# Two-layer graph attention on one core: the head's order of x, W and wh, and who makes the low parts in the two closings

## The reference, cut to what matters

```python
def layer(x, W, adj):                    # x (4096, 256), W (256, 512), adj (4096, 4096)
    Wh, Ws = split(x @ W, 2, axis=-1)
    a = softmax(Wh @ Ws.T, axis=-1) * adj
    return leaky_relu(a @ Wh + x, 0.01)
y = x
for l in range(2):
    y = layer(y, W_stack[l], adj)
out = layernorm(x + y)                   # over the last axis, eps 1e-5
```

## Time and profile before

| what | us |
|---|---|
| median of 3 runs | 1600.88 (1599.6 to 1602.52) |
| the profiled execution | 1602.16, span 1600.4 |
| TensorE busy | 1556.9 (97% of the span) |
| VectorE busy | 1349.2 (84%) |
| GpSimd busy | 800.8 (50%) |
| ScalarE busy | 646.9 (40%) |
| mean granted TensorE clock | 0.994 |

### The profile page before, as it was taken

One profiled execution on the slowest core, in us unless ns is written; L12 is line 12 of the kernel. 1 busy time (PEld: TensorE's weight loads), 2 busy tenths in 40 slices (PEclk: granted clock), 3 DMA queues, 4 the chain that ended last, 5 costly groups with the idle time before them and its releaser, 6 DMA issues.

```text
span 1600.4 us, 23327 instructions
## 1 busy us (share of the span) xinstructions
PE 1556.9 (97%) x8104; PEld 1320.4 (83%) x8104; DVE 1349.2 (84%) x1569; ACT 646.9 (40%) x1175; POOL 800.8 (50%) x801
## 2 busy tenths in 40 slices
PE   6999999999999999999899999999999999999996
PEld 6888888888888888888787888888888888888875
DVE  4688778877887788788847899999999999999988
ACT  4344444344444444443434444443344444444432
POOL 0055555555555555555422555555555555555554
PEclk9999999999999999999899999999999999999999
DMA  5277767676777777678924777787777777777784
GB/s 190 75 189 192 198 184 201 185 202 188 199 191 197 195 192 200 190 200 210 240 92 120 197 194 211 191 202 189 206 197 205 197 207 198 194 208 195 203 221 119
DMA packets 166981, 302.57 MB, mean 189 GB/s; under 512 B 39760, under 2 KB 67408, under 8 KB 166736
## 3 DMA queue, kind: packets, MB, share of 16 engines
q1 hardware_dynamic: 104896, 131.97, 32.6%
q0 software_dynamic: 37200, 135.28, 29.6%
q10 hardware_dynamic: 24768, 33.85, 7.8%
HBM read 157.29 MB, written 9.44 MB: 104 GB/s over the span
## 4 chain that ended last, share of the span: by engine, by line
PE 88%; DVE 6%; DMA 2%; issue 1%; SPq 1%; ACT 1%; POOL 1%; ACTq 0%; POOLq 0%
PE banks L634 27%; PE banks L521 16%; PE banks L523 15%; PE banks L522 15%; PE banks L636 14%; DVE ring L958 2%; SPq L348 1%; DVE ring L963 1%; DVE x_t L894 1%; DVE neg_max L930 1%; DMA turned<-ring 1%; POOL a_lo L1128 1%; DMA ring<-x_scratch 0%; PE banks L564 0%; ACT ring L764 0%
## 5 line engine op out<-in xcount | busy, mean ns | idle before, releaser
L1128 POOL TENSOR_TENSOR a_lo<-turned,a_hi 128x512 fp32r<-128x512 f32 x488 | 627.4, 1301 | 626.1 <-ACT a_hi L785 624.2
L634 PE MATMUL banks<-wh,a_hi 128*128 128x512 f32 x1952 | 700.0, 398 | 7.1 <-POOL a_lo L1128 6.9
L764 ACT ACTIVATE ring<-banks,neg_max 128x1024 f32<-128x1024 f32 x256 | 286.1, 1118 | 850.0 <-DVE neg_max L930 839.0
L636 PE MATMUL banks<-wh,a_lo 128*128 128x256 f32 x1952 | 548.8, 281 | 0.0
L930 DVE TENSOR_REDUCE neg_max<-banks 128x1 f32<-128x1024 f32 x256 | 311.9, 1219 | 166.8 <-PE banks L523 166.8
L634 PEld LDWEIGHTS banks<-wh,a_hi 128*128 128x128 f32 x1952 | 367.8, 188 | 96.9 <-POOL a_lo L1128 7.1
L521 PE MATMUL banks<-x_t,q_t 128*128 128x512 f32 x1024 | 407.7, 398 | 6.8 <-DVE q_t L894 6.8
L523 PE MATMUL banks<-x_t,q_t 128*128 128x512 f32 x1024 | 402.9, 393 | 0.0
L522 PE MATMUL banks<-x_t,q_t 128*128 128x512 f32 x1024 | 401.0, 392 | 0.0
L636 PEld LDWEIGHTS banks<-wh,a_lo 128*128 128x128 f32 x1952 | 369.4, 189 | 7.9
L958 DVE SCALAR_TENSOR_TENSOR ring<-ring,weight,load 128x1024 f32<-128x1024 f32 x254 | 328.4, 1293 | 0.8 <-DMA load<-adj 0.7
(11 more groups left out here) (81 smaller groups left out, 895.7 us busy)
## 6 DMA issues: line engine op xcount, KB each, us to landing
load<-adj POOLq DMA_DIRECT2D x254, 512.0 KB, 5.1
turned<-ring SPq DMA_DIRECT2D x1504, 64.0 KB, 4.0
turned<-ring ACTq DMA_DIRECT2D x496, 64.0 KB, 3.2
ring<-x SPq DMA_DIRECT2D x8, 512.0 KB, 5.8
rows<-x SPq DMA_DIRECT2D x32, 128.0 KB, 3.4
x_scratch<-rows SPq DMA_DIRECT2D x32, 128.0 KB, 2.9
rows<-x_scratch SPq DMA_DIRECT2D x30, 128.0 KB, 3.5
first_rows<-x SPq DMA_DIRECT2D x30, 128.0 KB, 3.1
```

The costliest lines, as they stand in the source:

```text
L634: nc.tensor.matmul(psum[:, bank, :], of_hi[:, b], wh[:, k].rearrange("p a d -> p (a d)"), start=start, stop=stop, skip_group_check=True)
L636: last = nc.tensor.matmul(psum[:, bank, 0:D], of_lo[:, b], wh[:, k, 0], start=False, stop=stop, skip_group_check=True)
L764: nc.scalar.activation(ring_at(i).rearrange("p (r b j) -> p b r j", r=2, j=QUAD), psum[:, 2 * (i % 2):2 * (i % 2) + 2, :].rearrange("p h ( ...
L1128: nc.gpsimd.tensor_tensor(operand(1, j).rearrange("p b (r j) -> p b r j", r=QUADS), as_f32(turned_in[unit_place(unit)][:, :, b:b + SUB, :] ...
```

## The change

Head: SyncE loads W of layer 0 and seven groups of x at once (two into `load`), the eighth when W's first half is split, W of layer 1 when group 4 has been turned. TensorE turns groups 0 to 5 through three pairs of banks with `q` 0 after group 2; groups 6 and 7 come after the first scores, W of layer 1 is turned in step 1 and its M made in step 2. Its parts lie in the last four tiles of `wh` until they are stored. GpSimd loads the first adj when groups 5 and 6 are turned. wh: two per step, in steps 0 to 7 (layer 0) and 4 to 7 (layer 1).

Closings: VectorE's low parts are 1, 2, 3, 5, 7 (layer 0) and 1, 2, 3 and the other odd ones (layer 1), each placed between a weighing and its turning. Chunk 125's maximum is taken before weigh 121, 126's before turn 122. GpSimd waits for weigh 124 before low 4, for weigh 125 before low 6, and for weigh 127 before low 8.

```diff
+        FIRST_BANKS = [0, 2, 6, 0, 2, 6, 2, 6]
+        FIRST_FREE = [0, 0, 0, 1, 2, 3, 5, 6]
-        LOW_BY_DVE = [(0, 1, 3), tuple(range(1, 16, 2))]
+        LOW_BY_DVE = [(1, 2, 3, 5, 7), (1, 2, 3, 5, 7, 9, 11, 13, 15)]
+        def head_at(step):
+            return {0: [("x", 6), ("x", 7)], 1: [("wt", 1)], 2: [("w", 1)]}.get(step, [])
-        WH_AFTER = [{0: 3, 1: 3, 2: 3, 3: 3, 4: 2, 5: 2}, {3: 3, 4: 3, 5: 2}]
+        WH_AFTER = [{n: 2 for n in range(8)}, {n: 2 for n in range(4, 8)}]
...
-            for g in range(2):
+            for g in range(GROUPS - 1):
                 load_x(g)
+            sp.wait_ge(wt_done, 1)
+            sp.wait_ge(w_lo, 1)
+            load_x(GROUPS - 1)
+            sp.wait_ge(xt_done, 5)
             load_w(1)
-            for g in range(2, 4):
-                load_x(g)
-            for g in range(4, GROUPS):
-                sp.wait_ge(xt_done, g - 3)
-                load_x(g)
...
             transpose_x(1)
-            pe.wait_ge(wt_lo, 1)
-            transpose_w(1)
             transpose_x(2)
-            make_m(1)
-            for g in range(3, GROUPS):
+            make_side(("q", 0))
+            for g in range(3, 6):
                 transpose_x(g)
-            pe.wait_ge(wt_lo, 2)
-            make_side(("q", 0))
...
                 scores(chunk_at(step))
+                for kind, n in head_at(step):
+                    if kind == "x":
+                        transpose_x(n)
+                    elif kind == "wt":
+                        pe.wait_ge(xt_lo, GROUPS)
+                        transpose_w(n)
+                    else:
+                        make_m(n)
...
-            def last_steps(end, last):
+            def last_steps(end, j, last):
                 weigh_and_turn(end - 9)
                 row_weights(last - 1)
                 chunk_max(end - 4)
                 weigh_and_turn(end - 8)
+                chunk_max(end - 3)
                 weigh_and_turn(end - 7)
-                chunk_max(end - 3)
-                weigh_and_turn(end - 6)
+                weigh(end - 6)
                 chunk_max(end - 2)
+                turn_blocks(end - 6)
+                weigh_and_turn(end - 5)
+                finish_rows(last - 3)
+                chunk_max(end - 1)
+                low_a(j + 1)
+                row_weights(last)
+                low_a(j + 2)
+                weigh(end - 4)
+                low_a(j + 3)
+                turn_blocks(end - 4)
+                weigh(end - 3)
+                low_a(j + 5)
+                turn_blocks(end - 3)
             def close_first():
...
-                low_a(j)
-                low_a(j + 1)
-                row_weights(TILES - 1)
-                weigh_and_turn(CHUNKS - 4)
-                low_a(j + 3)
-                weigh_and_turn(CHUNKS - 3)
                 split_x(8)
-                weigh_and_turn(CHUNKS - 2)
+                weigh(CHUNKS - 2)
+                low_a(j + 7)
+                turn_blocks(CHUNKS - 2)
                 weigh_and_turn(CHUNKS - 1)
             def close_second():
...
-                weigh_and_turn(end - 4)
-                low_a(j + 3)
-                weigh_and_turn(end - 3)
-                low_a(j + 5)
-                weigh_and_turn(end - 2)
-                low_a(j + 7)
+                weigh(end - 2)
+                low_a(j + 7)
+                turn_blocks(end - 2)
                 weigh_and_turn(end - 1)
...
-            pool.wait_ge(w_next_stored, 32)
             for i in range(2):
+                pool.wait_ge(xt_done, GROUPS - 2 + i)
                 load_adj(nc.gpsimd, i)
...
             def close_first():
-                split_a(j + 2)
+                split_a(j)
                 load_next_x(10)
                 load_last_adj(end)
-                for n in range(4, 12):
+                for n in (4, 6):
+                    pool.wait_ge(a_done, end - 4 + n // 2 - 1)
                     split_a(j + n)
                 pool.wait_ge(a_done, end)
+                for n in (8, 9, 10, 11):
+                    split_a(j + n)
...
             def close_second():
                 split_a(j)
-                split_a(j + 2)
                 load_last_adj(end)
-                split_a(j + 4)
-                split_a(j + 6)
+                for n in (4, 6):
+                    pool.wait_ge(a_done, end - 4 + n // 2 - 1)
+                    split_a(j + n)
                 load_late_rows()
+                pool.wait_ge(a_done, end)
                 split_a(j + 8)
```

More of the change, by code:

```diff
@@ L310, in gat_layernorm @@
             last_in[side_bank[s]] = side_place[s]
-        x_rows = [ring[:, g % 4, :] for g in range(GROUPS)]
+        x_rows = [ring[:, n, :] for n in (0, 1, 2, 3, 5)] + [load[:, 0, :], load[:, 1, :], ring[:, W_SLOT, :]]
         x_rows += [as_f32(q_t[:, p]).rearrange("p a k n -> p (a k n)") for p in range(2)]
@@ L317, in gat_layernorm @@
         x_rows += [ring_at(X_CHUNK[14]), ring_at(X_CHUNK[15])]
-        x_place = [g % 4 for g in range(GROUPS)] + [4 + g for g in range(GROUPS)]
+        x_place = list(range(2 * GROUPS))
         def x_count(g):
@@ L546, in transpose_x @@
             def transpose_x(g):
-                pair = X_BANKS[g] if g >= GROUPS else 2 * (g % 2)
+                pair = X_BANKS[g] if g >= GROUPS else FIRST_BANKS[g]
                 pe.wait_ge(x_loaded[x_place[g]], x_count(g))
@@ L592, in make_side @@
                         pe.wait_ge(xt_lo, layer * GROUPS + (half + 1) * GROUPS // 2)
+                    if not layer and bank >= ACC_BANK:
+                        pe.wait_ge(w_lo, 4)
                     if layer and bank >= ACC_BANK:
@@ L887, in _ @@
                 exponentials(chunk_at(step))
+                for kind, n in head_at(step):
+                    {"x": split_x, "wt": split_wt, "w": split_w}[kind](n)
                 for side in sides_after(step):
@@ L897, in split_wt @@
                 dve.wait_ge(wt_hi, layer + 1)
[L898 removed]
+                low(w_t[layer][1], wt_banks[layer], w_t[layer][0]).then_inc(wt_lo, 1)
             def split_w(layer):
@@ L904, in split_w @@
                 dve.wait_ge(w_hi, 2 * layer + 2)
-                low(w_made[layer][1][:, :, D:2 * D], psum[:, ACC_BANK + layer, :].rearrange("p (k e) -> p k e", k=KT),
+                low(w_made[layer][1][:, :, D:2 * D], m_banks[layer].rearrange("p (k e) -> p k e", k=KT),
                     w_made[layer][0][:, :, D:2 * D]).then_inc(w_lo, 1)
             def split_x(g):
-                pair = X_BANKS[g] if g >= GROUPS else 2 * (g % 2)
+                pair = X_BANKS[g] if g >= GROUPS else FIRST_BANKS[g]
                 dve.wait_ge(xt_hi, g + 1)
@@ L1004, in _ @@
             split_x(1)
-            split_wt(1)
             split_x(2)
-            split_w(1)
-            for g in range(3, GROUPS):
+            split_side(("q", 0))
+            for g in range(3, 6):
                 split_x(g)
-            split_side(("q", 0))
             def low_a(j):
```

54 lines of the change are left out of this document (25 added, 29 removed).

## The result

Over 20 runs each, the changed kernel took a median of 1598.13 us (1595.18 to 1601.33) and the kernel before 1601.91 (1597.74 to 1607.36): ratio 0.9976, 95% interval 0.9966 to 0.9986, or 3.8 us less (2.2 to 5.4), more than the 3.2 that can be told from no change. The sum had -3.9. The total came out, but two parts of it did not, and they failed in opposite directions: the head and wh brought more than forecast, the closings cost where a gain was forecast.

What follows compares the result with a forecast made beforehand. It took TensorE's waits (about 43 us idle) and the half-rate stretches behind them as the bound; -5.5 + 1.6 + 1.0 - 2.7 + 1.7 = -3.9 from 1600.88 gave 1597.0 us, range 1589.5 to 1603.

Steps and rivals of the forecast that it cites:

- The head: Before the first scores: TensorE's waits on VectorE fall from 6.3 to 0.8 us, -5.5 us.
- wh: First products of each layer: VectorE falls behind with two wh per step, +1.6 us in layer 0, +1.0 in layer 1.
- the 0.4 added for a weighing caught behind GpSimd: Layer 0's first products: GpSimd's subtraction might catch weigh 3, 1.3 us more; waits of 5.1 taken as 5.5.
- The first closing: End of layer 0: earlier maxima, moved low parts and spaced GpSimd subtractions let turn 127 end sooner, -2.7 us.
- that one is the 4.49 us wait: First closing: VectorE's low 3 standing through four GpSimd subtractions (4.95 us) was taken as TensorE's 4.49 us wait.
- the closing gains what turn 127 gains: First closing: an earlier turn 127 passes on through 11 DMA issues and x, 1.4 to 4.0 us.
- 4.4 us cap: First closing: DMA engines, busy at 0.89 over 40 us, have only 4.4 us of slack, which limits the gain.
- That the spacing would do nothing: Rival, both closings: GpSimd's condition for low 6 is already met, closings come out as before; -2.9, 1598.0 us; chance 0.12.
- The last closing: End of layer 1: low 5 and 7 ahead of turns delay the chain behind ScalarE's DMA issues, +1.7 us, bounds -3 and +4.
- The rounds: Last closing: DMA issue, high parts, GpSimd, low part and turn in sequence, 5.9 us to turn 125, 6.4 to turn 126.
- I let 1 us come back: Last closing, behind turn 127: 1 us regained because VectorE's row statistics no longer stand ahead of low 13.
- The rival with the other sign: Last closing: low 5 and 7 wait out another subtraction, last products at half clock, closing +7.1; total +4.2, 1605.1; chance 0.13.

Runs made afterwards that it cites:

- run 1: Changed kernel with VectorE's and GpSimd's closing orders and the low-part table of the kernel before, so new head and wh only: 1595.43 us, ratio 0.9958.
- run 2: Kernel before with only the two new closings and their table of VectorE's low parts; head and wh as before: 1603.80 us, ratio 1.0013.
- run 6: Changed kernel with VectorE's low 5 and low 7 behind the turns of chunks 125 and 126, last closing only: 1592.38 us, ratio 0.9946.
- run 3: Kernel before, unchanged, profiled a second time: one execution of 1600.58 us.
- run 10: Changed kernel with both closings as before the change and layer 1's wh in three steps as before: 1595.24 us, ratio 0.9957.
- Run 12: Changed kernel loading only two of four blocks of each group of layer 1's x, so computing with stale numbers: 1594.86 us, ratio 0.9956.
- run 5: Changed kernel without GpSimd's waits for VectorE's weighings ahead of its low parts in both closings: 1596.38 us, ratio 0.9966.
- run 7: Changed kernel without GpSimd's spacing waits and with low 5 and low 7 behind the turns in the last closing: 1594.19 us, ratio 0.9952.
- run 8: Changed kernel with layer 1's wh made in steps 3 to 5 (3, 3, 2) as before: 1595.26 us, ratio 0.9957.

## Why the prediction was right in its sum and wrong in two of its terms

By runs 1 and 2 the head and wh bring 6.7 us where the prediction had 2.9 (-5.5 + 1.6 + 1.0), and the closings cost 2.1 where it had a gain of 1.0 (-2.7 + 1.7). The sum was right because these errors, 3.8 and 3.1 us, have opposite signs. That is luck.

**1. The head: -5.5, held.** Where TensorE has its full clock early (last section), the first scores start at 17.3 us (17.34 in run 6; forecast 17.6) with 0.64 us of waiting ahead of them. Maximum 11 then starts at 93.3 us (93.24 to 93.43 in four profiles) against 98.51 before; taking out the 0.4 us that layer 0's wh cost, the head is worth 5.6. But the profile it was priced against had the best head of three: maximum 11 came at 99.49 in the second profile of before and at 101.43 in run 2, which has before's head. Over all profiles, whatever the clock did, maximum 11 comes at 99.8 with the old head (3) and at 94.5 with the new one (11), 5.3 us apart. Less the 1.2 that layer 1's wh cost (point 2) that makes 4.1 of run 1's 6.7 (4.6 to 9.0 by its interval); the rest is not located.

**2. wh: mechanism right, layer 0 mis-sized.** VectorE falls behind as described (maxima 5 to 8 at 56.02, 62.65, 70.86, 79.11: 6.6, 8.2 and 8.3 us apart). In layer 0 the waits sum to 4.32 where I took 5.5, against 3.89 before: +0.4 and not +1.6. The largest part is the last wait, 0.49 + 1.02 for a forecast 1.9; the 0.4 added for a weighing caught behind GpSimd was not needed, although weigh 3 was caught (2.20 us). In layer 1 the new spread took 49.4 to 49.5 us in all seven profiles; the old one 47.76 to 50.16, mean 48.3: +1.2 against the forecast +1.0.

**3. The first closing: -2.7, not confirmed.** The first failed step is to count "that one is the 4.49 us wait" as a gain: I took a wait of one profile for a property of the order. Run 3 has the same order without it, and so have runs 1 and 10. The other case, the weighing of 3.32 us, does belong to the old order (3.31 to 3.33 in all four profiles) and is gone with the new one: TensorE's wait there fell from 2.15 to 1.84 and 1.48 in the two profiles of after (1.1 to 2.8 in all with the new order), where I kept 1.2, and in the last closing from 2.16 to 1.10, where I kept 0.9. The second is "the closing gains what turn 127 gains". Turn 127 did end sooner (784.80 against 792.47: 4.5 us, once the 3.2 by which the stage starts sooner are taken off). Counted from maximum 123, it comes at 45.3 us on average with the old order (4 profiles) and at 43.1 with the new one and its spacing (7), a gain of 2.2 against a forecast 2.7; but from there to maximum 131 it is 46.3 and 47.9 us, and 1.6 of the gain is gone. The averages stay far under the 4.4 us cap. The means over the profiles are 91.6 us for the old order (4) and 91.0 for the new one with its spacing (7), a difference of 0.6 in a scatter of 5.9. TensorE's clock makes part of the scatter: in this stage it stood at the 1.2 GHz level for 10.2 us in the longest profile of the old order (93.75 us) and not at all in the shortest (88.84). A straight-line fit over all 14 profiles, an estimate, gives the stage's length within 0.4 us as 79.6 us + 1.15 times TensorE's idle time + 0.39 times its time at the lower level. By these rows the new order has 2.7 us less at the lower level on average (2.4 against 5.1) but no less idle time (9.1 against 8.6): it did not shorten TensorE's waits at all. Run 12 shows one bound there behind another. That the spacing would do nothing was a rival with 0.12; runs 5 and 7 bear its mechanism out, and its time (1598.0) was as near to the median as the forecast's.

The rule of the Trainium skill that was weighed there (SBUF — State Buffer, section SBUF: two separate sides: the pair is held for one whole instruction) describes run 3: low 3 got in after one of four subtractions. It does not account for the earlier trace rows, where low 3 took 5.15 us past three such boundaries; that VectorE would be let in at the first of them was the prediction's reading. So the traces bear out both outcomes. The distance of the starts does not decide it: in run 1 it was 0.35 us, and low 3 took 1.51. What does stays open.

**4. The last closing: +1.7, mis-sized; +3.3 by the profiles.** The rounds were right. Wrong was what stood beside them. "I let 1 us come back": nothing came back; behind turn 127 the kernel after took 19.45 and 20.81 us to VectorE's end, and before 19.99 and 19.98. Over all profiles with low 5 and 7 ahead (7) and with the old order (4) the 3.3 us are -1.7 up to turn 124 (forecast -1.8), +4.5 from there to turn 127 (forecast +4.2) and +0.4 behind it (forecast -1.0). (The terms of the first round, given as 5.9, add to 5.8.) And the one profile of before had a closing of 64.62 where three others with that order had 62.96, 62.31 and 61.87 (mean of the four 62.9; of the seven profiles with low 5 and 7 ahead 66.3). Runs 6 and 7 show the cause: those two low parts ahead of the turns, alone undone, give all 3.3 us back and more (60.93 to 62.34). The rival with the other sign had the place right (0.13); its 7.1 us were too many, since each low part waited out one subtraction (1.40 us) and no more.

What that rival also had, half clock at the last products, did come. Windows from 1560 to 1580 us of the kernel before, the kernel after and run 6:

```profile
1560.00:1580.00 20.00, 15.14 (x82) 12.23 (x82) 18.82 (x22) 6.93 (x13) 9.05 (x10) 1.00 0.71 182
1560.00:1580.00 20.00, 12.64 (x45) 10.13 (x44) 14.05 (x18) 5.07 (x9) 7.71 (x9) 0.75 0.56 152
1560.00:1580.00 20.00, 14.96 (x72) 12.27 (x72) 17.91 (x28) 6.82 (x12) 11.89 (x12) 0.91 0.60 145
```

Between maximum 251 and its last matmul TensorE stood at the 1.2 GHz level for 3.4 us or less in the seven profiles with these low parts behind the turns, for 10.2 us in five of the seven with them ahead, and for 13.7 in the other two, which have the longest last closings (66.93 and 67.32). In the kernel after they begin where waits of 3.07, 2.11 and 2.18 us for low parts end. How much of the 3.3 us is the turns' and how much the clock's no run separates, since the one brings the other.

**Best version.** Run 6: the change with two instructions of VectorE behind the turns instead of ahead, 8.7 us under its own runs of before by its ratio (5.9 to 11.4). Neither taking out the spacing nor putting layer 1's wh back improved on it; the three versions lie within each other's intervals, and these overlap those of runs 1, 8 and 10, so the choice among them rests on the stages.

## What to carry to other kernels

Price a stage against several executions when its waits come from engines that can fall together in more than one way: steady stages agreed within 0.03 us here, while the closings scattered by up to 6 us with the same order. A share moved to an engine that has time must not be put ahead of the step that releases the next round; behind it two instructions cost nothing that could be told, ahead of it 3.3 us. And where a wait goes away, ask which resource ends the stage next: here VectorE stood close behind the DMA engines. And look at TensorE's clock in the stage, in every profile: a few us of waiting can bring a stretch at the lower level, and such stretches account for part of the scatter.

## What the runs showed that I had not expected

- TensorE's full clock came at one of two moments. Windows of the kernel after, and then of run 6:

```profile
9.00:11.00 2.00, 1.78 (x8) 1.78 (x9) 1.52 (x3) 1.14 (x2) 0.00 (x0) 1.00 1.10 373
11.00:13.00 2.00, 2.00 (x11) 2.00 (x11) 0.65 (x2) 0.60 (x1) 0.00 (x0) 1.00 1.10 346
```
```profile
9.00:11.00 2.00, 1.79 (x15) 1.79 (x16) 1.78 (x3) 0.92 (x3) 0.00 (x0) 1.00 1.10 358
11.00:13.00 2.00, 2.00 (x21) 2.00 (x20) 1.01 (x3) 1.73 (x3) 0.00 (x0) 1.00 1.10 347
```

  As busy, with half as many matmuls. The windows show a clock of 1.00 only because the record of the granted clock is empty there: its first entry, at 1.00 (the 2.4 GHz level), comes at 13.65 us in the kernel after and at 7.88 in run 6. Up to that moment the matmuls of 128 columns start 0.21 us apart, from it on 0.11, as they do at 0.50 (the 1.2 GHz level) and 1.00 elsewhere. This is so in all 14 profiles: TensorE begins at the lower level, does 16 matmuls from 4.8 to 8.6 us, waits, and goes on. In six profiles the rise came at 7.9 to 8.8 us, in eight only at 12.6 to 14.3, and then the 12 matmuls of the first M and some behind them ran at the lower level: 1.9 us on average on everything behind, by maximum 0 of the new head (21.9 to 22.7 us in seven profiles, 20.3 to 20.5 in four). One of three profiles with the old head had it too (33.10, not 30.9), so it belongs to no one kernel. It is why the first scores of the kernel after came at 19.38. What decides between the two moments stays open.
- GpSimd and VectorE hold each other up in two ways with the same code: one engine through all four subtractions of the other (5.15 us), or in turns (1.53 and 2.30 us).
- The stage means add up to less than the measured 3.8: -5.3 (maximum 11, all profiles of either head) + 1.2 - 0.6 + 3.3 = -1.4. With a first closing that scatters by 6 us and four profiles of the old order the sum of means is no closer than that; the timed runs 1 and 2 carry the verdict, the stages only its place.
